# A vision tower in three stages: bias rows through TensorE, a new order of steps, later folds

## The reference

```
x   = patches @ W_tok + b_tok                          # 768 -> 256
s_t = a * s_(t-1) + dt*(B x_t + b_B)                   # state-space scan over the 196 patches of an image
y   = C s + b_C + D x + b_D                            # + residual, LayerNorm
h1  = x + y (normalised inputs around it);  x2 = LayerNorm(h1)
q,k,v = x2 @ w_in.T + b_qkv ; attention over the 64 images for each patch, 4 heads of 64
z   = x2 + softmax(q k / 8) v @ w_o.T + b_o            # post-norm: y1 = LN(z) * g1 + be1
gates = softmax(y1 @ wg); expert = argmax of 8; gate value of it
keep a token only if it is among the first S/8 tokens of its expert
ffn = (y1 @ w1[e]) @ w2[e] + b2[e]                     # 256 -> 1024 -> 256, no nonlinearity between
out = h1 + LN(y1 + gate * ffn) * g2 + be2
```

## Time and profile before

| | |
|---|---|
| median of 3 runs | 1268.35 us (1265.66 to 1270.06) |
| the profiled execution | 1266.32 us |
| its span, first to last instruction | 1264.4 us, mean granted PE clock 0.973 |
| busy: PE / weight loads | 1134.3 us (90%) / 1030.8 us (82%) |
| busy: DVE / POOL / ACT | 1000.9 (79%) / 886.2 (70%) / 776.5 us (61%) |
| first stage | up to about 540 us |
| second stage | 540 to 1059 us |
| third stage | 1059 to 1264 us |

### The profile page before, as it was taken

The page is one execution under the profiler, slowest core; times in us unless marked ns, Lnnn a source line. Parts: engine busy times, 40 slices in busy tenths (PEclk is TensorE's granted clock), DMA queues, the critical chain, the costliest instruction groups (busy, mean ns, idle before and its releaser), DMA issues. The chain is left out here.

```text
span 1264.4 us, 36668 instructions
## 1 busy us (share of the span) xinstructions
PE 1134.3 (90%) x10938; PEld 1030.8 (82%) x10939; DVE 1000.9 (79%) x2811; ACT 776.5 (61%) x1714; POOL 886.2 (70%) x1193
## 2 busy tenths in 40 slices
PE   1999999999999999879988889898989874999994
PEld 1999999999999999778888888888888863666662
DVE  5588888888888888727977777777777767799997
ACT  3465555666566666447766666666666651678875
POOL 1566767666666677216888888888888884478887
PEclk9999999999999999989999999999999977999997
DMA  7435545454554553212333333333333325788882
GB/s 216 174 129 159 165 154 175 149 184 149 169 169 146 174 159 118 100 34 86 111 110 100 104 106 107 104 108 104 101 111 104 106 87 178 214 232 237 243 235 90
DMA packets 97312, 180.22 MB, mean 143 GB/s; under 512 B 12319, under 2 KB 62753, under 8 KB 96226
## 3 DMA queue, kind: packets, MB, share of 16 engines
q1 hardware_dynamic: 82500, 138.66, 36.4%
q0 software_dynamic: 13312, 39.75, 8.6%
q10 hardware_dynamic: 1440, 1.07, 0.3%
HBM read 112.69 MB, written 67.80 MB: 143 GB/s over the span
## 5 line engine op out<-in xcount | busy, mean ns | idle before, releaser
L528 POOL TENSOR_TENSOR xl<-xf,xh 128x512 fp32r<-128x512 f32 x141 | 184.9, 1339 | 167.8 <-ACT xh L447 167.8
L311 PE MATMUL ps_h<-wh,xh 128*128 128x256 f32 x588 | 165.7, 282 | 4.9 <-DVE xl L669 4.9
L311 PE MATMUL ps_h<-wh,xl 128*128 128x256 f32 x588 | 166.6, 283 | 0.0
L311 PE MATMUL ps_h<-wl,xh 128*128 128x256 f32 x588 | 166.5, 283 | 0.0
L1475 POOL DMA_INDIRECT out<-res,c_idx x106 | 124.1, 1171 | 43.0 <-issue 21.1
L1084 POOL DMA_INDIRECT bins<-rows,slot_i x98 | 101.7, 1038 | 59.1 <-POOL slot_i L1078 40.0
L1623 PE MATMUL c_ps_y<-w,yt 128*128 x424 | 118.2, 401 | 2.7 <-ACT c_py L1430 1.1
L311 PE MATMUL b<-x2h,wh 128*128 128x256 f32 x392 | 117.5, 300 | 2.6 <-DVE x2l L1102 1.8
L311 PEld LDWEIGHTS ps_h<-wh,xh 128*128 128x128 f32 x588 | 112.2, 191 | 5.7 <-DVE xl L669 5.7
L311 PE MATMUL b<-x2h,wl 128*128 128x256 f32 x392 | 113.5, 289 | 0.0
L311 PE MATMUL b<-x2l,wh 128*128 128x256 f32 x392 | 113.3, 289 | 0.0
(11 more groups left out here) (282 smaller groups left out, 4290.7 us busy)
## 6 DMA issues: line engine op xcount, KB each, us to landing
xf<-xt SPq DMA_DIRECT2D x49, 768.0 KB, 5.4
row<-bins SPq DMA_DIRECT2D x106, 257.5 KB
h_dram<-h1b SPq DMA_DIRECT2D x49, 256.0 KB, 5.5
x_dram<-x2o SPq DMA_DIRECT2D x49, 256.0 KB, 5.6
x<-x_dram SPq DMA_DIRECT2D x98, 128.0 KB, 2.7
rows<-h_dram SPq DMA_DIRECT2D x98, 128.0 KB
w1s<-w1t SPq DMA_DIRECT2D x8, 1024.0 KB, 6.8
w2s<-w SPq DMA_DIRECT2D x8, 516.0 KB, 5.9
```

The source lines that it names most:

```text
L311: last = nc.tensor.matmul(out_ps, a, b, start=(i == 0), stop=(i == len(terms) - 1))
L528: last = nc.gpsimd.tensor_tensor(xl[:, p, part], xf[:, p, part], xh[:, p, part].bitcast(F32), ALU.subtract)
```

## The change: what it does

Bias through TensorE. `two_rows` and `b12s` become 128 rows, and a new `bo_s` holds b_o and the gate's constant in the same way: hi in row 0, lo in row 32, zeros elsewhere. In `project` a matmul with `two_rows` and `bo_s` opens each of the two products; POOL's x2b, xg2 and `split_bias` go, DVE's residual reads x2 itself. The split of b12 moves into the first stage: ACT's b12s in slot 1, `low_bias` on DVE in slot 2, and four operations for `bo_s` ahead of the last `g_lo`.

Input in six buffers: x2 is `[P, XB, 2, D]`, XB = 6, and SP waits for `turn_x` and the residual of the group six before.

New orders in the second stage, of PE, ACT, DVE and POOL, with `scores` of k-2, `turn_e` and `attend` of k-3 and `rank` of k-5, so one step more in the pipeline; the loop of SP also has six steps now.

Late folds. Experts 5 and 6 (LATE) are not folded in the first stage, whose loop ends at step 24 instead of 42 (what is behind it is unrolled). Their weights, 4 x 1 MB, are loaded in steps 3 and 4 of the second stage; PE makes the quarters between the last steps of it.

Early table. POOL's iota, the constants and the table of the first 16 tiles are made in the second stage, behind `fi`; the other 90 at the start of the third. SP loads the first eight pairs before those. One scan over 784 elements with restarts replaces 8 scans. Idle matmuls are 12 instead of 40.

Norm in two steps. In the third stage ACT's `norm` and DVE's `c_nm` go. DVE computes (z - mean) * g2 with two SCALAR_TENSOR_TENSOR (`centre`) and then * (1/deviation) + row with two more (`finish`). `keep` works on two pairs at once.

```diff
+FIRST = 2 * DEPTH
...
+LATE = (5, 6)
+IDLE = 12
...
+LO = 32
+RB = LO + 2
+XB = 6
...
-        b12 = sb("b12", [2, NE, D])
-        b12s = sb("b12s", [2, NE, D], F32R)
-        two_rows = sb("two_rows", [2, P], F32R)
-        half = sb("half", [2, 2])
+        b12 = sb("b12", [RB, NE, D])
+        b12s = sb("b12s", [P, NE, D], F32R)
+        bo_s = sb("bo_s", [P, D + NC], F32R)
+        two_rows = sb("two_rows", [P, P], F32R)
...
+        def tables(v, link, lo, hi):
+
+            count, c = hi - lo, slice(lo, hi)
+            link(v.tensor_tensor(ge[:, c], tix[:, c].unsqueeze(2).to_broadcast([P, count, NE]),
+                                 nt[:, 2, :].unsqueeze(1).to_broadcast([P, count, NE]), ALU.is_ge))
+            v.tensor_tensor(gw[:, c], ge[:, c], nt[:, 3, :].unsqueeze(1).to_broadcast([P, count, NE]), ALU.mult)
+            link(v.tensor_reduce(tile_e[:, c], ge[:, c], AX_X, ALU.add))
+            link(v.tensor_reduce(tile_r[:, c], gw[:, c], AX_X, ALU.add))
+            link(v.scalar_tensor_tensor(tile_r[:, c], tix[:, c], float(P), tile_r[:, c], ALU.mult, ALU.add))
+            v.tensor_scalar(tab_e[:, c], tile_e[:, c], float(NE - 1), None, ALU.min)
+            return v.tensor_scalar(tab_r[:, c], tile_r[:, c], float(BINS), None, ALU.min)
...
+                    if k.slot(FOLD) == 1 and k.back(2).valid(FOLD * NE):
+                        e = k.turn(FOLD) - 1
+                        wait(act, fb_out, e + 1)
+                        nc.scalar.activation(b12s[0:RB, bass.ds(e, 1), :].rearrange("p a d -> p (a d)"),
+                                             b12[:, bass.ds(e, 1), :].rearrange("p a d -> p (a d)"),
+                                             ACT.Copy).then_inc(fb_hi, 1)
+                run(act, step, 0, NG + 5, 6, FOLD * (LATE[0] - 1), FOLD)
...
+                def low_bias(k):
+                    if k.slot(FOLD) == 2 and k.back(3).valid(FOLD * NE):
+                        e = k.turn(FOLD) - 1
+                        wait(dve, fb_hi, e + 1)
+                        row, two = (a[LO:RB, bass.ds(e, 1), :].rearrange("p a d -> p (a d)") for a in (b12, b12s))
+                        v.tensor_tensor(two, row, two.bitcast(F32), ALU.subtract)
...
+                bo_f = scratch(D + NC)[0:RB]
+                v.tensor_copy(bo_f[:, 0:D], r_bo[0:RB]).then_inc(bo_split, 1)
+                dve.wait_ge(sums_out, 1)
+                v.tensor_copy(bo_f[:, D:], g_bo[0:RB]).then_inc(bo_split, 1)
+                dve.wait_ge(bo_split, 2)
+                v.tensor_copy(bo_s[0:RB], bo_f).then_inc(bo_split, 1)
+                dve.wait_ge(bo_split, 3)
+                v.tensor_tensor(bo_s[LO:RB], bo_f[LO:RB], bo_s[LO:RB].bitcast(F32), ALU.subtract).then_inc(bo_split, 1)
...
-                    p = m.slot(2)
-                    wait(sp, Q["x2T"], m.n() - 1)
-                    wait(sp, Q["x2b"], m.n() - 1)
+                    p = m.slot(XB)
+                    wait(sp, Q["x2T"], m.n() + 1 - XB)
+                    wait(sp, Q["z"], m.n() + 1 - XB)
...
-                    for m, stage in ((k.back(3), et_out), (k.back(4), squares), (k.back(3), o_hi), (k.back(2), exps),
-                                     (k.back(1), lambda m: qk_out(m, "q_ps", q, 0, "q_out")), (k.back(5), e_log),
-                                     (k.back(1), lambda m: qk_out(m, "k_ps", kk, FT, "k_out")), (k.back(4), z_norm),
-                                     (k.back(1), xg_out), (k.back(1), v_out), (k, x_hi)):
+                    for m, stage in ((k.back(2), exps), (k.back(1), lambda m: qk_out(m, "k_ps", kk, FT, "k_out")),
+                                     (k.back(1), lambda m: qk_out(m, "q_ps", q, 0, "q_out")), (k, x_hi),
+                                     (k.back(4), z_norm), (k.back(1), v_out), (k.back(1), xg_out), (k.back(2), et_out),
+                                     (k.back(3), squares), (k.back(4), e_log), (k.back(2), o_hi)):
...
-                    for m, stage in ((k.back(4), y1), (k.back(4), send), (k, add_const), (k, add_bias), (k.back(2), rstd),
-                                     (k.back(2), centre), (k.back(3), count)):
+                    for m, stage in ((k, centre), (k.back(2), send), (k, rstd),
+                                     (k.back(1), y1), (k.back(1), count)):
...
-                    v.tensor_tensor(z[:], b_z[:, :, 0:D], x2b[:, p], ALU.add).then_inc(Q["z"], 1)
+                    v.tensor_tensor(z[:], b_z[:, :, 0:D], x2[:, p], ALU.add).then_inc(Q["z"], 1)
...
-                    for m, stage in ((k.back(5), gates), (k.back(2), normalise), (k.back(4), expert),
-                                     (k.back(3), residual), (k.back(3), gate_sum), (k, x_lo), (k.back(1), softmax),
-                                     (k.back(4), place), (k.back(4), scaled), (k.back(2), o_lo), (k.back(3), logits),
-                                     (k.back(3), shift), (k.back(3), top_logit)):
+                    for m, stage in ((k.back(2), softmax), (k.back(5), place), (k.back(3), o_lo), (k.back(2), normalise),
+                                     (k.back(4), shift), (k.back(4), logits), (k, x_lo), (k.back(5), gates),
+                                     (k.back(3), gate_sum), (k.back(3), residual), (k.back(4), top_logit),
+                                     (k.back(4), scaled), (k.back(4), expert)):
...
+                        mm(b_z[:, s, 0:D + NC], two_rows[:], bo_s[:], start=True, stop=False)
                         last = product(b_z[:, s, 0:D + NC],
                                        [(both(oh_, ol_, slice(None), slice(t * G + s * P, t * G + (s + 1) * P)),
                                          both(wh, wl, slice(None), slice(W_OUT + t * OS, W_OUT + (t + 1) * OS)))
-                                        for t in range(FT)])
+                                        for t in range(FT)], first=False)
...
-                    for m, stage in ((k.back(1), queries), (k.back(1), keys), (k.back(1), values), (k.back(3), project),
-                                     (k, turn_x), (k.back(2), turn_e), (k.back(1), scores), (k.back(2), attend),
-                                     (k.back(4), rank)):
+                    for m, stage in ((k.back(3), turn_e), (k.back(1), keys), (k.back(2), scores), (k.back(3), attend),
+                                     (k.back(5), rank), (k.back(1), queries), (k.back(1), values), (k, turn_x),
+                                     (k.back(3), project)):
...
+                def late_fold(quarter):
+                    i, part, again = quarter // 4, quarter // 2 % 2, quarter % 2
+                    if quarter == 0:
+                        pe.wait_ge(wx_loaded, 4 * 16)
+                        pe.wait_ge(Q["k_out"], 2 * NG)
+                    if quarter == 4:
+                        pe.wait_ge(late_out, 1)
+                    for f in range(again * FK // 2, (again + 1) * FK // 2):
+                        last = mm(b_4[:, part * D:(part + 1) * D], w1x[:, i, f * D + part * P:f * D + (part + 1) * P],
+                                  w2x[:, i, f * D:(f + 1) * D], start=(f == 0), stop=(f == FK - 1))
+                    if quarter % 4 == 3:
+                        last.then_inc(late_ps, 1)
+
+                run(pe, step, 0, NG + 1, 6, 48, FOLD)
+                late_fold(0)
+                step(At(0, NG + 1, FOLD))
+                late_fold(1)
+                step(At(0, NG + 2, FOLD))
+                late_fold(2)
+                late_fold(3)
+                for c in range(NG + 3, NG + 5):
+                    step(At(0, c, FOLD))
+                late_fold(4)
                 pe.wait_ge(Q["acc"], 2 * NG)
-                pe.wait_ge(Q["k_out"], 2 * NG)
-                mm(b_4[:, 0:NE], ones_b[:], oh_acc[:], start=True, stop=True).then_inc(cnt_ps, 1)
+                pe.wait_ge(Q["et_out"], NG)
+                mm(b_1[:, 0:NE], ones_b[:], oh_acc[:], start=True, stop=True).then_inc(cnt_ps, 1)
+                for quarter in range(5, 8):
...
+                def centre(k):
                     p = k.slot(2)
+                    wait(dve, mv_s, k.n() * 2 + 2)
+                    for i in range(2):
+                        v.scalar_tensor_tensor(zg[:, p, i, :], z[:, p, i, :], mv[:, p, i, 0:1], r_g2, ALU.subtract,
+                                               ALU.mult).then_inc(zg_s, 1)
...
+                    for i in range(2):
+                        last = v.scalar_tensor_tensor(res[:, b, i, :], zg[:, p, i, :], rs[:, p, i:i + 1], row[:, b, i, D:2 * D],
+                                                      ALU.mult, ALU.add)
+                    last.then_inc(res_s, 1)
...
-                for _ in range(40):
+                for _ in range(IDLE):
```

284 lines of the change are left out of this document (131 added, 153 removed).

## The result

The changed kernel takes 1249.6 us (1246.66 to 1251.3, 4 runs) against 1268.48 for the kernel before beside it: ratio 0.985, interval [0.9826, 0.9874]. Forecast were 1229 us, 39 us less; it became 19 us less. The profiled execution took 1246.66 us with a span of 1244.9.

A forecast was written before the change was run, and what follows sets the result against it. PE was taken to bound the first stage, POOL's 9.94 us round the second, PE and DVE nearly full in the third. Terms -16.6 + 0.5 + 1.3 - 28 - 1 + 0 + 4 = -39.8 gave 1229 us, range 1199 to 1259.

The forecast's parts named there:

- fewer folds in the first stage: First stage: leaving out experts 5 and 6 saves 8 quarters of 1.77 us and three loop ends, -16.6 us.
- Preamble and end of the first stage: First stage's two ends: small linked operations add +0.5 us in the preamble and +1.3 before the barrier.
- The second stage's period: Second stage: POOL's relief shortens the step from 9.97 to 9.35 us (PE's floor 8.65), -28 us over 46 steps.
- term of 0.7 for held signals: Second stage: signals held while POOL issues DMAs cost 0 to 1.7 us a step; 0.7 was taken.
- Rival (a): Second stage: no signal is held, period 8.7 us, 58 us less instead of 28, total 1199 us; chance 0.15.
- Rival (b): Second stage: PE's instruction supply sets the pace, not POOL; period 10.1 us, +6 instead of -28, total 1263; chance 0.10.
- (c): Second stage: the scores' signal always falls into the held stretch, period 10.8 us, total 1295 us; chance 0.07.
- Late weights: Second stage: 4 MB of late weights in two of SP's steps cost nothing, as DMA is a third busy.
- Drain: End of the second stage: late folds mostly fit PE's gaps and a drain step is shorter, -1 us (-4 to +8).
- Start of the third stage: Early tile table wins about 1 us, PE at a lower clock costs at most 2; both together 0.
- Third stage: Third stage: DVE's four new operations against those it loses cost +0.08 us a pair, +4 us over 53 pairs (-8 to +16).
- rival (d): Third stage: the four new DVE operations are paid in full, +16 us, total 1241 us; chance 0.08.

The follow-up runs named there:

- a3: The kernel with the later bias load, its seven accumulating bias sums on DVE narrowed to 8 of 256 columns (biases wrong): 1225.02 us.
- a4: The kernel with the later bias load, POOL's subtraction xl made in six operations of half the width instead of three: 1226.68 us.
- a1: The changed kernel with the load of expert biases into 34 partitions moved behind the first weights and patches on SP's queue: 1235.95 us.
- b4: The kernel before with lighter POOL work only: x2b for 16 of 256 columns, only the first copy of the bias split (output wrong): 1229.69 us.
- b1: The changed kernel with experts 5 and 6 folded in the first stage again and the second stage's old orders of PE, ACT, DVE, POOL: 1300.95 us.
- b2: b1 with xg in six buffers instead of two: 1259.7 us.
- m6: m4 with the four 1 MB late-weight loads in SP's steps 42 to 45 instead of two each in steps 3 and 4: 1220.06 us.
- m4: The changed kernel with the later bias load, xl in six pieces and the third stage's old norm; late folds stay: 1224.03 us.
- c1: The changed kernel with the third stage's norm as before; keep still takes two pairs at once: 1230.58 us.
- a2: The changed kernel with experts 5 and 6 folded in the first stage again, no late weights or late quarters: 1277.77 us.
- m3: a5 with the third stage's old norm: 1222.46 us.
- a5: a2 with the later bias load and PE's second stage written out instead of a loop of six steps: 1238.2 us.
- m5: m3 with POOL's xl in six pieces: 1227.55 us.

## Why the prediction was wrong, point by point

**The step that failed** is "fewer folds in the first stage: -16.6, between -12 and -18". The count of quarters, their 1.77 us and the three loop ends are not what failed. Wrong was "PE is the only full engine there": DVE at 84 to 88 of 100 us was next behind, with bias sums that stay when the folds go, and taking PE's work away moved DVE's two-source instructions under POOL's `xl`, which stretched them. The stretch, without the preamble, became 1.2 us shorter instead of 16.6. DVE's 86.0 of 100 us in the kernel before, in steps of 10.2 on average, are by my estimate 8.8 us of work a step: next to nothing is left of a step of 8.92, and less in the four of six that have the bias sums. a3 and a4 show it from both sides: give DVE back 0.65 us in four steps of six, or halve POOL's operations that it waits for, and 10 us come (471.8 to 461.4 and 461.5). The share of "DVE turns out next" was in the text, as a bound of -12 that took DVE's busy time as fixed; a row of the kernel before spoke against that, an operation that takes 0.67 elsewhere, and I used the rule for the second stage only:

```profile
L581 DVE TENSOR_TENSOR sl<-xs,sh 128x512 fp32r<-128x512 f32 x44 | 65.1, 1480 | 0.0
```

**Missed altogether:** the load of b12 into 34 partitions, +7.8 us with what stands behind it (a1 gives 6.6 back). I counted the instructions that the change adds on DVE and none of what it adds on SP's queue ahead of the first weights.

**Preamble and end of the first stage:** +0.5 and +1.3 forecast, 0.5 (29.4 against 28.9 for the first patch matmul) and 0.2 measured.

**The second stage's period:** right in mechanism, too careful in size. POOL did pace it (b4: 38 us from lighter POOL alone) and the floor of PE, 8.65, was nearly met: 8.89 instead of 9.35, -45 us instead of -28. If the floor of 8.65 was right, the term of 0.7 for held signals is 0.24. The prediction tied these waits to the phase in which the engines settle; b4 loses them by POOL's relief alone, and b1 and b2, in the old orders too, have none. That a DMA of POOL stops PE's small matmuls holds for `attend` (39 of 39), not for `scores` (0 of 44). Rival (a) had the right picture and too low a floor. Rival (b), that the orders and PE's supply set the pace, falls with b4; its 10.1 turned up in b1 for another reason. (c) did not occur; a single `mx` in the drain starts 1.6 us late.

**Late weights** "cost nothing": the first nine steps became 3.2 us longer. Moving the loads takes 5.7 us off them and adds 2.5 behind (m6 against m4); the kernels without late weights take 75.2 to 76.8 us there.

**Drain:** -1 forecast with an end of +8; +9.8 in the profiled execution. About 4 stay in the good drains (a1, c1). They are not the quarters' doing, since kernels without them take 40.5 to 42.6 us (a2, m3, a5, m5). b2, with the old orders and depth, takes 37.3, which points at the new orders with their deeper pipeline. The other 6 go with the broken burst of `attend`, whose cause stays open.

**Start of the third stage:** 0 forecast, -2.6 measured.

**Third stage:** +4 forecast, +9.6 measured, about halfway to rival (d)'s +16. The four operations cost 0.40 us each start to start, 1.59 together, at the lower end of my bounds. But I set 1.66 against them by busy times. Start to start `zg`, `res` and `nm` are 0.59, 0.58 and 0.19, which is 1.36, and the rest of the change gains 0.05 (c1). 1.59 - 1.41 is +0.18 a pair, and 53 pairs make 9.6. The padded bias rows, priced "as any other" from mean durations, in fact took 0.3 us a tile off PE.

Sum of the misses: first stage 22.7, drain 11, third stage 5.6 and first steps 3 one way; steady steps 17, start of the third stage 3, its end 1 and the end of the first stage 1 the other.

## What to carry to other kernels

Before taking work from a full engine, ask which engine stands next and whether its busy time will stay what it is: in this kernel DVE's instructions with two SBUF sources lasted as long as the POOL operation beside them (`nm_z` 0.19 or 1.26 us), and a shift of phase alone made the same step 10.5 us in the changed kernel and 11.7 in a1. Look for the engine whose round has no gap, not for the one with the largest busy share, and test it by making its work lighter: one run settled what the profile could only suggest. Don't take two traces' difference in a drain for the edit's: 6 us came and went between kernels whose drains are the same program. Count what an edit adds to a queue, and where in the queue, as strictly as what it adds to an engine.
